# First cross-attention: parts of keys and queries kept in DRAM, core in chunks of four heads

## The chip, the cores and the metric

One core of a Trainium2 chip runs the kernel. The metric is the device time of one execution in microseconds; the time before is the median of three runs. The profile is one further execution.

## What is computed

A decoder of two layers on x of shape (2, 512, 512), each layer with self-attention, cross-attention to a context of shape (2, 1024, 512), and a mixture of experts. The change is in the cross-attention of the first layer:

```python
q = _qdq(x) @ _qdq(wq).T + bq            # int8 fake-quantised rows
kv = cond @ wkv.T + bkv
k, v = jnp.split(kv, 2, axis=-1)          # 16 heads of 32, 1024 keys, 512 queries, 2 batches
attn = jax.nn.softmax(jnp.einsum('bnhd,bmhd->bhnm', q, k) * scale, axis=-1)
o = jnp.einsum('bhnm,bmhd->bnhd', attn, v).reshape(B, N, C)
out = _qdq(o) @ _qdq(wp).T + bp
```

## The kernel before

The kernel is written engine by engine: SP, TensorE (pe), ScalarE (act), VectorE (dve) and GpSimd (pool) each have their own list of instructions in the order of the source, and wait for each other through counting semaphores. Every stage (`Stage`) ends with a barrier of all engines. The stages of the first cross-attention are `project_cross0` (projection), `attention_core` (the core) and `output_cross0` (output).

The projection makes keys transposed (`kt`, 128 rows of head features by 1024 keys, for each of 8 blocks of four heads), values (`v`), and queries (`qt`). Four context chunks of 512 tokens are multiplied by the key weights (L1025) and the value weights (L1033). Between them VectorE rounds the rows of the weights and of the normalised input (jobs, `round_rows`), ScalarE turns them into bf16 integers (L984), and after all four chunks TensorE transposes the 16 of them (L1041), ScalarE copies each away (L988), diagonal matmuls spread the scales (L1048), and the queries follow (L1057, L968, L1012). Keys are taken out of PSUM by L978, values by L937. Beside each head's 32 columns of values lie 32 columns of ones, written once, so that a matmul of 64 columns gives the weighted values and the sums of weights of one head.

Scores must be exact to more than float32r, so keys and queries are split into a high part (float32r, ScalarE, L704) and a low part (the rest, GpSimd, L746), and a score matmul contracts 96 rows: high by high, low query by high key, high query by low key. DMAs (L580 on SP for queries, L757 on GpSimd for keys) gather for each head these 96 rows from `parts` into `packed`, six transfers of each kind for a pair of heads; slots for four pairs exist.

The core then runs over 16 pair chunks j. First the maxima: `piece(j, n)` are two matmuls of 128 queries by 1024 keys of one head (L639), reduced by VectorE (`top`, L785), two pairs of PSUM banks taking turns. When eight are reduced, `turn` transposes the negated maxima (L645), ScalarE and VectorE make high and low rows of them (L710, L791), and SP puts the rows under the packed queries (L587, four transfers), beside rows of ones in the keys. So a second matmul (`scores`, L656, 98 rows, keys by queries) yields score minus maximum, ScalarE exponentiates (L718), and `values` (L668) multiplies with values and ones, two heads side by side in 64 columns each. In step kb of chunk j TensorE does the scores of block kb for two heads, the values of block kb-1, and one piece of chunk j+2. At the end of a chunk ScalarE copies the bank out (`take`, L724), SP moves values into `ot` and sums into `total` (L598, L599), and after every second chunk VectorE takes the reciprocal of 512 columns (L797) and multiplies (L799). VectorE's order is: top(j+2, 0), row(j+1), the other tops of j+2, then `norm` of the block before.

Of the kernel before, what the change touches and what calls it, by code (L numbers as in the profile page):

```python
# [15 lines left out]
P = 128  # L16
# [4 lines left out]
H = 16  # L21
# [492 lines left out]
def attention_core(nc, g, st, qt, kt, v, ot, nkt, masks=None):  # L514

    causal = masks is not None
    NI, NP, QB = B * KC, B * KC * HPC // 2, S // P
    NK = nkt * P
    KB = NK // S
    SLOTS = 4
    PB = 2 if causal else 1
    RING = 8
# [3 lines left out]
    parts = [st.sbuf(f"parts{n}", [P, 2 + 2 * KB, S], F32R) for n in range(PB)]  # L533
    packed = st.sbuf("packed", [P, SLOTS, 2, 1 + KB, S], F32R)
    probs = g.xt[:, :, :].rearrange("p k (a n) -> p (k a) n", n=S)
    nmax = st.sbuf("nmax", [P, 2, 2 * QB])
    rows = st.sbuf("rows", [2 * QB, 2, 2, P], F32R)
    osb = st.sbuf("osb", [P, 2, S])
    total = st.sbuf("total", [P, S])
    mask16 = st.sbuf("mask16", [P, P], BF16) if causal else None  # L540
    high_done, low_done = st.sem("high_done"), st.sem("low_done")
    packed_in = [st.sem(f"packed_in{n}") for n in range(SLOTS)]
    keys_in = [st.sem(f"keys_in{n}") for n in range(SLOTS)]
    rows_in = [st.sem(f"rows_in{n}") for n in range(2)]
    early_ones_done, late_ones_done = st.sem("early_ones_done"), st.sem("late_ones_done")
    mask_done = st.sem("mask_done")
# [4 lines left out]
    spread = [st.sem(f"spread{n}") for n in range(2)]  # L551
    inverted, normed = st.sem("inverted"), st.sem("normed")

    def high(u):
        t = parts[u % PB]
        return t[:, 0, :], t[:, 2:2 + KB, :].rearrange("p a n -> p (a n)")

    def low(u):
        t = parts[u % PB]
        return t[:, 1, :], t[:, 2 + KB:2 + 2 * KB, :].rearrange("p a n -> p (a n)")  # L560

    def piece_bank(j, n):
        return 2 * (((nkt + 1) * j + n) % 2)

    def start_of(kb):
        return kb * P if causal else 0

    with nc.Block() as block:
        @block.sync
        def _(sp):  # L570
            def pack(j):
                u, s = j // 2, j % SLOTS
                sp.wait_ge(low_done, 2 * u + 2)
                if j >= SLOTS:
                    sp.wait_ge(st_made, 2 * nkt * (j - SLOTS + 1))
                t = parts[u % PB]
                for h in range(2):
                    a = (2 * (j % 2) + h) * DH
                    for r, (qp, kp) in enumerate(TERMS):
                        sp.dma_start(packed[r * DH:(r + 1) * DH, s, h, 0, :].bitcast(F32),  # L580
                                     t[a:a + DH, qp, :].bitcast(F32)).then_inc(packed_in[s], 16)

            def put_rows(j):
                sp.wait_ge(row_low, j + 1)
                for n in range(2):
                    for h in range(2):
                        sp.dma_start(packed[KR + n:KR + n + 1, j % SLOTS, h, 0, :].bitcast(F32),  # L587
                                     rows[h * QB:(h + 1) * QB, j % 2, n, :].bitcast(F32)).then_inc(rows_in[j % 2], 16)

            def lay(j):  # L590
                i = j // 2
                sp.wait_ge(taken, j + 1)
                if j % 2 == 0 and i >= 1:
                    sp.wait_ge(normed, i)
                for h in range(2):
                    a = (2 * (j % 2) + h) * DH
                    val, ones = (3 if h else 0) * DH, (1 + h) * DH
                    sp.dma_start(ot[a:a + DH, i, :], osb[val:val + DH, j % 2, :]).then_inc(spread[j % 2], 16)  # L598
                    sp.dma_start(total[a:a + DH, :], osb[ones:ones + DH, j % 2, :]).then_inc(spread[j % 2], 16)  # L599

            for j in range(SLOTS):
                pack(j)
            put_rows(0)
            for j in range(NP):
                if j >= 1 and j + SLOTS - 1 < NP:
                    pack(j + SLOTS - 1)
                if j + 1 < NP:
                    put_rows(j + 1)
                if j >= 1:
                    lay(j - 1)  # L610
            lay(NP - 1)
            for n in range(2):
                sp.wait_ge(spread[n], 64 * NP // 2)

        @block.tensor
        def _(pe):
            def piece(j, n):
                s, bank = j % SLOTS, piece_bank(j, n)
                if n == 0:
                    pe.wait_ge(packed_in[s], PACK * (j // SLOTS + 1))  # L620
                    pe.wait_ge(keys_in[s], PACK * (j // SLOTS + 1))
                    if j >= 1:
                        pe.wait_ge(max_done, nkt * j)
                elif n == 1:
                    if j >= 1:
                        pe.wait_ge(row_low, j)
                else:
                    pe.wait_ge(max_done, nkt * j + n - 1)
                if causal:
                    w = (n + 1) * P  # L630
                    for h in range(2):
                        nc.tensor.matmul(g.ps[:, bank + h, 0:w], packed[0:KR, s, h, 0, n * P:(n + 1) * P],
                                         packed[0:KR, s, h, 1, 0:w], start=True, stop=False)
                        mm = nc.tensor.matmul(g.ps[:, bank + h, n * P:w], g.ident16[:, :], mask16[:, :], start=False,
                                              stop=True)
                else:
                    h, qb = divmod(n, QB)
                    for a in range(KB):
                        mm = nc.tensor.matmul(g.ps[:, bank + a, :], packed[0:KR, s, h, 0, qb * P:(qb + 1) * P],  # L639
                                              packed[0:KR, s, h, 1 + a, :], start=True, stop=True)  # L640
                mm.then_inc(max_made, 1)

            def turn(j):
                pe.wait_ge(max_done, nkt * (j + 1))
                nc.tensor.transpose(g.ps[0:2 * QB, piece_bank(j, nkt), 0:P], nmax[:, j % 2, :],  # L645
                                    g.ident[:, :]).then_inc(row_turned, 1)

            def scores(j, kb, h):
                s, e = j % SLOTS, 2 * (nkt * j + kb) + h
                if kb == 0 and h == 0:  # L650
                    pe.wait_ge(rows_in[j % 2], 64 * (j // 2 + 1))
                if e >= 2:
                    pe.wait_ge(exp_done, e - 1)
                a = start_of(kb)
                c = kb % QB * P
                mm = nc.tensor.matmul(g.ps[:, 4 + h, a:S], packed[0:KR + 2, s, h, 1 + kb // QB, c:c + P],  # L656
                                      packed[0:KR + 2, s, h, 0, a:S], start=True, stop=not causal)
                if causal:
                    mm = nc.tensor.matmul(g.ps[:, 4 + h, a:a + P], mask16[:, :], g.ident16[:, :], start=False, stop=True)
                mm.then_inc(st_made, 1)  # L660

            def values(j, kb):
                e, a = 2 * (nkt * j + kb), start_of(kb)
                pe.wait_ge(exp_done, e + 2)
                if kb == 0 and j >= 2:
                    pe.wait_ge(taken, j - 1)
                for h in range(2):
                    nc.tensor.matmul(g.ps[2 * h * DH:2 * (h + 1) * DH, 6 + j % 2, a:S],  # L668
                                     v[:, j // (H // 2), kb, j % (H // 2), h:h + 2, :].rearrange("p a d -> p (a d)"),
                                     probs[:, (e + h) % RING, a:S], start=(kb == 0),  # L670
                                     stop=(kb == nkt - 1)).then_inc(pv_made, 1)

            if causal:
                pe.wait_ge(mask_done, 1)
            for n in range(nkt):
                piece(0, n)
            turn(0)
            for n in range(nkt):
                piece(1, n)
            pe.wait_ge(early_ones_done, 1)  # L680
            pe.wait_ge(late_ones_done, 1)
            for j in range(NP):
                for kb in range(nkt):
                    scores(j, kb, 0)
                    scores(j, kb, 1)
                    if kb == 0 and j + 1 < NP:
                        turn(j + 1)
                    if kb >= 1:
                        values(j, kb - 1)
                    elif j >= 1:  # L690
                        values(j - 1, nkt - 1)
                    if j + 2 < NP:
                        piece(j + 2, kb)
            values(NP - 1, nkt - 1)

        @block.scalar
        def _(act):
# [1889 lines left out]
```

## Time and profile before

| | us |
|---|---|
| median of three runs | 3433.76 (3432.29 to 3434.08) |
| profiled execution, its own time | 3445.77 |
| its span, first to last instruction | 3444.0 |
| stretch of the projection's block to the first instruction of the core | 300 to 435.65 |
| first scores of the core | 476.09 |
| mean granted TensorE clock over the span | 0.92 |

TensorE is busy for 86% of the span, VectorE for 37%, ScalarE and GpSimd for 29% each. Busy times are averages over six stages of a different nature; only the second of them is touched, and it is read from its own stretches. A granted clock of 1.0 is 2.4 GHz, 0.5 is 1.2 GHz.

### The profile page before, as it was taken

The page shows a single profiled execution, that of the slowest core. Times are in us where ns is not written, and L with a number is a line of the kernel's source. Part 1 is how long each engine was busy: PE and PEld are TensorE (multiplying, and loading weights), DVE is VectorE, ACT ScalarE, POOL GpSimd, SP SyncE. Part 2 cuts the span into 40 slices and gives each one's busy share as a digit, 9 for nine tenths or more (in the row PEclk, how much of TensorE's full clock was granted, in tenths as well). Part 3 has the DMA queues.
Part 4 walks back from the last instruction along what each step waited for, and adds up shares of the span by engine and source line. Part 5 has one row for each costly group of instructions (what it writes and reads, how often), then busy time and mean ns, then how long its engine had stood idle before and what let it go on. Part 6 is the DMA issues. An engine that isn't in the chain of part 4 may idle for free. (4 is left out here: it accounts for less than half of the span.)

```text
span 3444.0 us, 42500 instructions
## 1 busy us (share of the span) xinstructions
PE 2962.6 (86%) x14027; PEld 1856.9 (54%) x14030; DVE 1291.0 (37%) x2069; ACT 1005.3 (29%) x2352; POOL 995.4 (29%) x1007
## 2 busy tenths in 40 slices
PE   7888969995399598799969899999999557999997
PEld 3453423333388345488848745555544424777772
DVE  3573355554111317554442265555540311111114
ACT  1461235443011126433310044444430001222220
POOL 2360032211211205244412055555540051221216
PEclk9999979997599799999989999999999677999998
DMA  2332033311199414144434332212210004999996
GB/s 83 76 73 89 13 82 72 71 41 34 61 328 322 139 42 96 46 156 140 140 110 144 95 125 76 74 64 76 76 37 0 28 18 145 346 342 339 345 305 197
DMA packets 308356, 434.40 MB, mean 126 GB/s; under 512 B 39871, under 2 KB 173479, under 8 KB 308233
## 3 DMA queue, kind: packets, MB, share of 16 engines
q1 hardware_dynamic: 273160, 348.88, 32.2%
q0 software_dynamic: 20096, 56.68, 5.9%
q10 hardware_dynamic: 14976, 27.27, 2.2%
q8 instruction: 69, 1.13, 0.1%
q14 instruction: 55, 0.44, 0.0%
HBM read 308.78 MB, written 75.58 MB: 112 GB/s over the span
## 5 line engine op out<-in xcount | busy, mean ns | idle before, releaser
L1586 PE MATMUL ps<-moe_blocks_xgt,moe_blocks_w 128*128 128x128 f32 (+1 forms) x3072 | 364.5, 277 | 6.2 <-DMA moe_blocks_b1s<-rb_cols 4.2
L1586 PEld LDWEIGHTS ps<-moe_blocks_xgt,moe_blocks_w 128*128 128x128 f32 (+1 forms) x3072 | 350.7, 185 | 10.8 <-issue 8.3
L2465 POOL TENSOR_TENSOR normed<-normed,xa_core_rinv 128x257 f32<-128x257 f32 (+1 forms) x256 | 265.8, 1061 | 273.2 <-DVE xa_core_rinv L2396 273.2
L1568 PE MATMUL ps<-moe_blocks_w,moe_blocks_ht 128*128 128x512 f32 (+1 forms) x624 | 285.0, 593 | 0.0
L2432 ACT ACTIVATE normed<-ps,xa_core_nmax 128x257 f32<-128x257 f32 (+1 forms) x256 | 173.6, 685 | 321.6 <-DVE xa_core_nmax L2391 321.1
L2391 DVE TENSOR_REDUCE xa_core_nmax<-ps 128x1 f32<-128x257 f32 (+1 forms) x256 | 164.5, 683 | 250.1 <-PE ps L2342 250.0
L2342 PE MATMUL ps<-xa_core_k,xa_core_q 128*128 128x512 f32 x512 | 242.3, 597 | 13.4 <-DVE xa_core_k L2381 11.6
L1657 DVE COPY moe_blocks_y<-ps 128x512 f32<-128x512 f32 x104 | 71.9, 691 | 454.9 <-PE ps L1568 454.9
L510 POOL TENSOR_TENSOR sa_w<-sa_w,sa_core_rinv 128x256 f32<-128x256 f32 (+3 forms) x128 | 159.2, 1253 | 239.5 <-DVE sa_core_rinv L457 239.5
L2368 PE MATMUL ps<-xa_core_pt,xa_core_v 128*128 128x512 f32 x512 | 225.1, 593 | 0.7 <-DVE xa_core_pt L2404 0.7
L785 DVE TENSOR_REDUCE xa_core_nmax<-ps 128x1 f32<-128x1024 f32 x128 | 155.9, 1223 | 138.1 <-PE ps L639 138.1
L718 ACT ACTIVATE normed<-ps 128x512 f32<-128x512 f32 x256 | 138.9, 595 | 160.1 <-PE ps L656 159.9
L2356 PEld LDWEIGHTS ps<-identity,normed 128*128 128x128 f32 x1024 | 118.2, 141 | 104.2 <-issue 67.8
L2121 POOL TENSOR_TENSOR normed<-normed 128x512 f32<-128x512 f32 x96 | 126.3, 1317 | 139.1 <-DVE normed L2081 139.1
L2356 PE MATMUL ps<-identity,normed 128*128 128x128 f32 x1024 | 146.3, 276 | 22.3 <-ACT xa_core_pt L2442 21.4
L1568 PEld LDWEIGHTS ps<-moe_blocks_w,moe_blocks_ht 128*128 128x128 f32 (+1 forms) x624 | 111.0, 191 | 100.2 <-issue 100.2
L1534 POOL COPY moe_blocks_idx<-moe_index 128x1 uint32 (+1 forms) x104 | 19.0, 183 | 490.2 <-PE ps L1559 437.2
L487 ACT ACTIVATE sa_w<-ps,sa_core_nmax 128x128 f32<-128x128 f32 (+3 forms) x256 | 132.2, 523 | 81.4 <-DVE sa_core_nmax L453 80.2
L1607 ACT ACTIVATE moe_blocks_xgt<-ps 128x512 f32<-128x512 f32 x104 | 62.1, 597 | 319.6 <-PE ps L1559 318.9
L2368 PEld LDWEIGHTS ps<-xa_core_pt,xa_core_v 128*128 128x128 f32 x512 | 95.0, 191 | 107.9 <-issue 107.0
L412 PE MATMUL ps<-identity,sa_w 128*128 128x128 f32 x640 | 122.0, 300 | 31.3 <-DVE normed L466 17.1
L668 PE MATMUL ps<-normed,xa_v 128*64 128x512 f32 x512 | 146.1, 651 | 0.0
(284 smaller groups left out, 5291.8 us busy)
## 6 DMA issues: line engine op xcount, KB each, us to landing
moe_blocks_w<-L_ffn_rw SPq DMA_DIRECT2D x80, 704.0 KB
moe_blocks_w<-L_ffn_rw SPq DMA_DIRECT2D x80, 512.0 KB
moe_blocks_w<-L_ffn_w SPq DMA_DIRECT2D x24, 1408.0 KB
moe_y<-moe_blocks_y ACTq DMA_DIRECT2D x104, 256.0 KB
sa_packed<-sa_parts SPq DMA_DIRECT2D x192, 128.0 KB
k_raw<-xa_kq_raw SPq DMA_DIRECT2D x64, 256.0 KB, 2.0
v_rows<-normed SPq DMA_DIRECT2D x64, 256.0 KB
xa_core_k<-k_raw SPq DMA_DIRECT2D x32, 512.0 KB, 4.7
```

The costliest lines, as they stand in the source:

```text
L510: nc.gpsimd.tensor_tensor(prob[:, 2 * s:2 * s + 2, 0:n], prob[:, 2 * s:2 * s + 2, 0:n], rinv[:, s, :, 0:1].to_broadcast([P, 2, n]), ALU.mu ...
L668: nc.tensor.matmul(g.ps[2 * h * DH:2 * (h + 1) * DH, 6 + j % 2, a:S], v[:, j // (H // 2), kb, j % (H // 2), h:h + 2, :].rearrange("p a d - ...
L718: nc.scalar.activation(probs[:, e % RING, a:S], g.ps[:, 4 + h, a:S], ACT.Exp).then_inc(exp_done, 1)
L785: nc.vector.tensor_reduce(nmax[:, j % 2, n:n + 1], g.ps[:, bank:bank + 2, :].rearrange("p a n -> p (a n)"), X_AXIS, ALU.max, negate=True). ...
L1568: mm = nc.tensor.matmul(g.ps[:, 6 + s % 2, :], ht[0:fn, s % 2, f, :], w2s[s][0:fn, f, :], start=(f == 0), stop=(f == NF - 1))
L1586: mm = nc.tensor.matmul(g.ps[0:fn, 2 + s % 2 + 2 * half, f * P:(f + 1) * P], w1s[s][:, k, half * F + f0:half * F + f0 + fn], xgt[:, s % 2, ...
L2342: mm = nc.tensor.matmul(s_ps(n)[:, c:c + 512], q[:, s, qb * P:(qb + 1) * P], k[:, s, c:c + 512], start=True, stop=True)
L2356: mm = nc.tensor.transpose(g.ps[:, 4 + half, m * P:(m + 1) * P], prob[:, nn % PR, c:c + P], g.ident[:, :])
L2368: mm = nc.tensor.matmul(g.ps[:, 6 + hs, :], v[:, hs, m, :], pt[:, hs, m, :], start=(m == 0), stop=(m == NKT - 1))
L2391: ins = nc.vector.tensor_reduce(nmax[:, n % PR, m:m + 1], s_ps(n)[:, lo:hi], X_AXIS, ALU.max, negate=True)
L2432: ins = nc.scalar.activation(prob[:, n % PR, lo:hi], s_ps(n)[:, lo:hi], ACT.Exp, bias=nmax[:, n % PR, m:m + 1], accum_out=rsum[:, n % PR, ...
L2465: ins = nc.gpsimd.tensor_tensor(prob[:, n % PR, lo:hi], prob[:, n % PR, lo:hi], rinv[:, n % PR, m:m + 1].to_broadcast([P, hi - lo]), ALU.mult)
```

## The change

The high and low parts are no longer made in the core. In the projection each key tile (one of 16) and query tile (one of 8) is written to `raw`, ScalarE copies it to `high`, GpSimd subtracts (`low`), all in rings of three, and SP stores both parts to DRAM (`k_parts`, `q_parts`). The last chunk's key and value matmuls are placed between the transposes. The core (`cross_core`) runs over 8 chunks of four heads. A chunk is loaded by six DMAs on SP, each with 32 rows for all four heads; there are three slots. Per block of keys there are four scores; the pieces of the next chunk, 16 of them, are placed three to a block. Values and totals use separate matmuls of 32 columns, four heads side by side, into two banks; ScalarE copies both out itself, and the reciprocal is cut into four and placed between reductions. The rows of maxima take two transfers instead of four. The rows of ones in the packed keys are written by GpSimd. `attention_core` was used only here and goes.

```diff
+def cross_core(nc, g, st, k_parts, q_parts, v, ot):
+    SLOTS = 3
+    STEPS = 2
+    PCS = HPC * QB
+    EACH = -(-PCS // (nkt - 1))
...
+            def pack(i):
+                s = i % SLOTS
+                if i >= SLOTS:
+                    sp.wait_ge(st_made, HPC * nkt * (i - SLOTS + 1))
+                for r, (qp, kp) in enumerate(TERMS):
+                    sp.dma_start(pq[r * DH:(r + 1) * DH, s, :, :].bitcast(F32),
+                                 q_parts[qp, i, :, :].rearrange("(h p) n -> p h n", p=DH)).then_inc(packed_in[s], 16)
+                    sp.dma_start(pk[r * DH:(r + 1) * DH, s, :, :].bitcast(F32),
+                                 k_parts[kp, i, :, :].rearrange("(h p) n -> p h n", p=DH)).then_inc(packed_in[s], 16)
...
+            pack(0)
+            pack(1)
             put_rows(0)
+            for i in range(NI):
+                if i + SLOTS - 1 < NI:
+                    pack(i + SLOTS - 1)
+                if i + 1 < NI:
+                    put_rows(i + 1)
...
+            def piece(i, m):
+                s, bank = i % SLOTS, piece_bank(i, m)
+                if m == 0:
+                    pe.wait_ge(packed_in[s], PACK * (i // SLOTS + 1))
+                    if i >= 1:
+                        pe.wait_ge(max_done, PCS * i)
+                elif m == 1:
+                    if i >= 1:
+                        pe.wait_ge(row_low, i)
                 else:
+                    pe.wait_ge(max_done, PCS * i + m - 1)
...
+                for h in (2 * pair, 2 * pair + 1):
+                    e = HPC * (nkt * i + kb) + h
+                    if e >= 2:
+                        pe.wait_ge(exp_done, e - 1)
+                    nc.tensor.matmul(g.ps[:, 4 + h % 2, :], pk[0:KR + 2, s, h, kb * P:(kb + 1) * P],
+                                     pq[0:KR + 2, s, h, :], start=True, stop=True).then_inc(st_made, 1)
...
+            def values(i, kb):
+                step = nkt * i + kb
+                b, c = divmod(i, KC)
+                pe.wait_ge(exp_done, HPC * step + HPC)
+                if kb == 0 and i >= 1:
+                    pe.wait_ge(taken, 2 * i)
+                for h in range(HPC):
+                    nc.tensor.matmul(g.ps[h * DH:(h + 1) * DH, 6, :], v[:, b, kb, c * P + h * DH:c * P + (h + 1) * DH],
+                                     probs[:, HPC * (step % STEPS) + h, :], start=(kb == 0), stop=(kb == nkt - 1))
+                for h in range(HPC):
+                    mm = nc.tensor.matmul(g.ps[h * DH:(h + 1) * DH, 7, :], g.ones[:, 0:DH],
+                                          probs[:, HPC * (step % STEPS) + h, :], start=(kb == 0), stop=(kb == nkt - 1))
+                mm.then_inc(pv_made, 1)
...
                 for kb in range(nkt):
+                    ahead = range(min(PCS, EACH * kb), min(PCS, EACH * (kb + 1))) if i + 1 < NI else ()
+                    if i == 0:
+                        for m in ahead:
+                            piece(i + 1, m)
+                    if kb == nkt - 1 and i + 1 < NI:
+                        turn(i + 1)
+                    scores(i, kb, 0)
+                    if i > 0:
+                        for m in ahead:
+                            piece(i + 1, m)
+                    scores(i, kb, 1)
                     if kb >= 1:
+                        values(i, kb - 1)
+                    elif i >= 1:
+                        values(i - 1, nkt - 1)
...
+                for m in range(PCS if i + 1 < NI else 0):
+                    top(i + 1, m)
+                    if i >= 1 and m in (6, 8, 10, 12):
+                        invert(i - 1, (m - 6) // 2)
+                    if i >= 1 and m == 14:
+                        norm(i - 1)
...
# project_cross0
+                sp.wait_ge(high_done, u + 1)
+                sp.dma_start(dst[0], high[:, u % HELD, :].bitcast(F32)).then_inc(stored[u % HELD], 16)
+                sp.wait_ge(low_done, u + 1)
+                sp.dma_start(dst[1], low[:, u % HELD, :].bitcast(F32)).then_inc(stored[u % HELD], 16)
...
+            for r in range(HELD):
+                sp.wait_ge(stored[r], 32 * len(range(r, UNITS, HELD)))
...
+            def held(u):
+                if u >= HELD:
+                    act.wait_ge(low_done, u - HELD + 1)
+                    act.wait_ge(stored[u % HELD], 32 * (u // HELD))
+                return raw[:, u % HELD, :]
+
+            def keep_high(u):
+                nc.scalar.activation(high[:, u % HELD, :], raw[:, u % HELD, :], ACT.Copy).then_inc(high_done, 1)
...
+                nc.scalar.activation(held(KU + j), qs[:, j % 2, :], ACT.Identity, bias=bqss[:, c:c + 1],
                                      scale=DH ** -0.5).then_inc(q_done, 1)
+                act.wait_ge(q_done, j + 1)
+                keep_high(KU + j)
...
+                if n % 2 == 0:
+                    if n // 2 < KC:
+                        key(NCH - 1, n // 2)
+                    else:
+                        value(NCH - 1, n // 2 - KC)
```

## Rows read from the trace of the kernel before

**Rows 1.** The page, part 1: busy us, share, instructions.
```profile
PE 2962.6 (86%) x14027; PEld 1856.9 (54%) x14030; DVE 1291.0 (37%) x2069; ACT 1005.3 (29%) x2352; POOL 995.4 (29%) x1007
```

**Rows 2.** The core's loop as one stretch: length, busy per engine (instructions), granted clock, DMA share, GB/s.
```profile
476.00:762.00 286.00, 262.53 (x913) 105.85 (x913) 163.13 (x139) 140.97 (x266) 56.61 (x84) 0.93 0.30 62
```

**Rows 3.** Groups by line, 300 to 1000 us: busy, mean ns, idle before.
```profile
L785 DVE TENSOR_REDUCE xa_core_nmax<-ps 128x1 f32<-128x1024 f32 x128 | 155.9, 1223 | 138.1 <-PE ps L639 138.1
...
L746 POOL TENSOR_TENSOR xa_core_parts<-xa_qt,xa_core_parts 128x512 fp32r<-128x512 f32 x8 | 10.1, 1267 | 216.3 <-ACT xa_core_parts L704 216.3
```

**Rows 4.** Timeline of one step: start, length, engine, line, operation, count, idle before.
```profile
559.94 0.74 PE L639 MATMUL ps<-xa_core_packed 96*128 96x512 f32 x2
...
560.52 0.63 PE L656 MATMUL ps<-xa_core_packed 98*128 98x512 f32 x2
560.72 1.23 DVE L785 TENSOR_REDUCE xa_core_nmax<-ps 128x1 f32<-128x1024 f32 x1 [0.93 <-PE ps L639]
...
560.75 0.40 PE L656 MATMUL ps<-xa_core_packed 98*128 98x512 f32 x1
...
560.95 1.08 ACT L718 ACTIVATE normed<-ps 128x512 f32<-128x512 f32 x2 [1.07 <-PE ps L656]
...
561.08 1.08 PE L668 MATMUL ps<-normed,xa_v 128*64 128x512 f32 x4
...
562.09 0.74 PE L639 MATMUL ps<-xa_core_packed 96*128 96x512 f32 x2
```

**Rows 5.** Timeline of a hand-over between two chunks.
```profile
572.62 3.34 DVE L797 RECIPROCAL xa_core_total<-xa_core_total 128x512 f32<-128x512 f32 x1
...
578.07 0.73 PE L639 MATMUL ps<-xa_core_packed 96*128 96x512 f32 x2 [1.90 <-DVE xa_core_rows L791]
```

**Rows 6.** Timeline of the start-up of the core.
```profile
452.06 2.08 PE L639 MATMUL ps<-xa_core_packed 96*128 96x512 f32 x4 [18.81 <-DMA xa_core_packed<-xa_core_parts]
...
463.35 0.08 PEld L645 LDWEIGHTS ps<-identity,xa_core_nmax 128*8 128x8 f32 x1 [2.03 <-DVE xa_core_nmax L785]
...
472.31 8.09 SPq L587 DMA_DIRECT2D xa_core_packed<-xa_core_rows  x5
...
476.09 1.19 PE L656 MATMUL ps<-xa_core_packed 98*128 98x512 f32 x2 [2.70 <-DMA xa_core_packed<-xa_core_rows]
```

**Rows 7.** Timeline of the projection's end; one row of line L1012 (min/median/max ns).
```profile
386.76 13.90 PE L1025 MATMUL ps<-xa_proj_ctx,xa_proj_wkv 128*128 128x512 f32 x32
...
394.03 0.63 ACT L984 ACTIVATE xa_proj_wp_int<-xa_proj_rounded 128x512 bf16<-128x512 f32 x1 [0.23 <-DVE xa_proj_rounded L929]
...
423.07 0.66 PE L1048 MATMUL ps<-xa_proj_diag,all_ones 128*128 128x128 f32 x4
...
L1012 ACT ACTIVATE xa_qt<-xa_proj_rounded,xa_proj_bqss x8: 721/722/723, 428.2 to 434.1; 128x512 f32<-128x512 f32 x8
...
435.65 0.63 ACT L704 ACTIVATE xa_core_parts<-xa_qt 128x512 fp32r<-128x512 f32 x1 [0.85 <-PEq L67]
```

**Rows 8.** Self-attention: the values of 32 columns, timeline; its whole stretch.
```profile
163.30 1.08 PE L429 MATMUL ps<-normed,sa_v 128*32 128x128 f32 x32
...
124.00:268.00 144.00, 119.76 (x1234) 80.88 (x1235) 102.31 (x200) 91.72 (x303) 79.60 (x64) 0.94 0.31 67
```

**Rows 9.** DMA issues (KB, us to landing); stretches as in rows 2.
```profile
k_raw<-xa_kq_raw SPq DMA_DIRECT2D x64, 256.0 KB, 2.0
...
444.00:447.00 3.00, 0.00 (x0) 0.00 (x0) 0.00 (x0) 0.00 (x0) 3.00 (x7) 0.50 0.99 194
447.00:450.00 3.00, 0.00 (x0) 0.00 (x0) 0.00 (x0) 0.00 (x0) 0.24 (x1) 0.50 1.02 246
...
300.00:305.00 5.00, 3.01 (x4) 1.49 (x5) 3.49 (x1) 0.00 (x0) 3.51 (x1) 0.50 1.05 406
```

**Rows 10.** Timeline of the core's end.
```profile
788.61 0.60 ACT L724 ACTIVATE xa_core_osb<-ps 128x512 f32<-128x512 f32 x1 [1.20 <-PE ps L668]
...
796.52 0.69 DVE L799 TENSOR_TENSOR xa_qt<-xa_qt,xa_core_total 128x512 f32<-128x512 f32 x1
```

More of the change, by code:

```diff
@@ L550, in attention_core, with piece_bank @@
     pv_made, taken = st.sem("pv_made"), st.sem("taken")
-    spread = [st.sem(f"spread{n}") for n in range(2)]
     inverted, normed = st.sem("inverted"), st.sem("normed")
[L554 to L566, printed above, removed]
+    def piece_bank(i, m):
+        return 2 * (((PCS + 1) * i + m) % 2)
     with nc.Block() as block:
@@ new lines, in piece @@
+            def piece(i, m):
[7 more added lines that the diff above has]
+                        pe.wait_ge(row_low, i)
+                else:
+                    pe.wait_ge(max_done, PCS * i + m - 1)
+                h, qb = divmod(m, QB)
+                for a in range(KB):
+                    mm = nc.tensor.matmul(g.ps[:, bank + a, :], pq[0:KR, s, h, qb * P:(qb + 1) * P],
+                                          pk[0:KR, s, h, a * S:(a + 1) * S], start=True, stop=True)
@@ L641, in piece, with turn @@
                 mm.then_inc(max_made, 1)
-            def turn(j):
-                pe.wait_ge(max_done, nkt * (j + 1))
-                nc.tensor.transpose(g.ps[0:2 * QB, piece_bank(j, nkt), 0:P], nmax[:, j % 2, :],
+            def turn(i):
+                pe.wait_ge(max_done, PCS * (i + 1))
+                nc.tensor.transpose(g.ps[0:HPC * QB, piece_bank(i, PCS), 0:P], nmax[:, i % 2, :],
                                     g.ident[:, :]).then_inc(row_turned, 1)
[L648 to L671, printed above, removed]
@@ L694, in _, with scores @@
-            values(NP - 1, nkt - 1)
+            def scores(i, kb, pair):
+                s = i % SLOTS
+                if kb == 0 and pair == 0:
+                    pe.wait_ge(rows_in[i % 2], 32 * (i // 2 + 1))
+                for h in (2 * pair, 2 * pair + 1):
[4 more added lines that the diff above has]
+                                     pq[0:KR + 2, s, h, :], start=True, stop=True).then_inc(st_made, 1)
@@ new lines, in row, with invert @@
+            def row(i):
+                dve.wait_ge(row_high, i + 1)
+                nc.vector.tensor_tensor(rows[:, i % 2, 1, :], g.ps[0:HPC * QB, piece_bank(i, PCS), 0:P],
+                                        rows[:, i % 2, 0, :], ALU.subtract).then_inc(row_low, 1)
+            def invert(i, n):
+                if n == 0:
+                    dve.wait_ge(taken, 2 * i + 1)
+                part = slice(n * P, (n + 1) * P)
+                nc.vector.reciprocal(total[:, part], total[:, part]).then_inc(inverted, 1)
@@ L864, in project_cross0 @@
     qs = rounded
+    raw, low = st.sbuf("raw", [P, HELD, S]), st.sbuf("low", [P, HELD, S], F32R)
+    high = st.sbuf("high", [P, HELD, S], F32R)
+    high_done, low_done = st.sem("high_done"), st.sem("low_done")
+    stored = [st.sem(f"stored{n}") for n in range(HELD)]
     w_loaded = [st.sem("wq_loaded"), st.sem("wp_loaded")]
```

383 lines of the change are left out of this document (140 added, 243 removed).

## The prediction

> **What bounds the kernel now.** I read the busy shares of the page first: TensorE is the busiest engine by far [rows 1]. Then the stretches of the stage that is changed. In the projection TensorE runs its matmuls without a gap (32 in 13.90 us [rows 7]); at the start-up of the core, to 476, the clock stands at 0.50, the lower level of 1.2 GHz [rows 9]; from 476 to 762 TensorE is busy for 92% at a mean clock of 0.93 [rows 2]. The groups by line give the unit costs that will be moved around [rows 3]. The timeline of one undisturbed step of the loop [rows 4] shows what sets its length: two score pieces begin at 559.94, two scores at 560.52, the value group at 561.08, the next pieces at 562.09. That is 2.15 us with TensorE never waiting; VectorE and ScalarE finish their part and sit idle. So the inner step is bound by TensorE, and every wait that the change puts into TensorE's queue is paid in full. The hand-over between two pair chunks is different: a 3.34 us reciprocal stands on VectorE ahead of the row that TensorE wants, and TensorE waits for it [rows 5]. Two more places lie on the path: the start-up, where packed keys arrive only at 452.06, then reductions set the pace, and the rows' transfers are issued only at 472.31 because the 24 transfers of queries stand ahead of them on SP [rows 6]; and the end of the projection, where queries leave at 0.82 us each [rows 7].
>
> Unit times I take from these rows. A float32r matmul of 512 columns: the next one starts 0.23 to 0.24 later (560.52, 560.75); the first after a float32 group or a wait takes 0.34 (0.58 less 0.24). From the start of the last matmul of a piece to its reduction 0.44, the reduction 1.22, back to TensorE 0.05. From a score to its exponential 0.43 (0.53 if it is the first), the exponential 0.60, a pitch of 0.5. Values of two heads: 1.01 for two passes of 0.43 side by side, with 0.15 for the start and the end.
>
> **Projection, moved work.** Each of 24 tiles (16 of keys, 8 of queries) now gets a high part on ScalarE (0.63, as L984 [rows 7]), a low part on GpSimd (1.27 [rows 3]) and two stores of 256 KB (2.0 us from issue to landing, the rows of the other DRAM buffer [rows 9]), in a ring of three. For keys this is hidden: a key tile comes every 3.43 us (eight records of 0.43 in [rows 7]), while the ring turns over in 0.72 + 0.63 + 1.27 + 0.15 for semaphores + 2.0 to 2.6 for issue and landing = about 5.1 us for three tiles. If that cover were gone, it would be 1.7 us a tile. For the eight queries nothing covers it: three tiles per 5.1 us, the last starting 11.6 us in and landing at 16.7, and SP waits for every store before the stage ends. Today the eight take 6.6 (428.2 to 434.8). So +10.1.
>
> The transposes are moved between the last keys and values. TensorE reaches them at 386.76. The third needs ScalarE's first copy, which stands behind the four roundings that end at 394.66 [rows 7]: a wait of 4.3 us. Then 16 transposes of 0.4 and 8 groups of 3.43 give 386.8 + 4.3 + 6.4 + 27.5 = 425.0, and the last value bias and the diagonals follow on VectorE before the row matmuls at 425.9, against 423.07 now: +2.8. The copies that used to pace the transposes are hidden, but their gain is eaten by the wait and by the diagonals that come late. The core stage then begins at 435.65 + 10.1 + 2.8 = 448.6.
>
> **Start-up of the core.** Removed: the high and low parts and 24 + 24 small transfers. Added: six loads for the first chunk, 3 x 256 + 3 x 512 KB = 2.36 MB, issued at once. Their rate is not in the trace in this form. Bounds: 194 to 246 GB/s when pairs are packed onto 32 partitions, 406 GB/s for wide loads from DRAM [rows 9]; 12 or 6 us. I take 225 GB/s, 10.5 us, since the 32 destination partitions and 2 to 4 KB pieces are the same as in the packing row. With 2.0 latency and 0.3 to begin, chunk 0 is there at 461.4 (now 452.06; the load itself is quicker than today's 16.4). Then 16 pieces run one behind the other, each 1.27 (eight take 11.3 until the transpose, [rows 6]): transpose at 482.8, row ready 1.0 later, two row transfers 2.6, first scores at 486.4. Today they start at 476.09. So +10.3: the 12.9 from the projection less 2.6. The Trainium skill, page DMA: Bandwidth & Descriptors (section Anatomy of one DMA), gives 2.0 us plus bytes at 436 GB/s; that would make it 7.4 us instead of 12.5, and the forecast 5 us lower. The packing row speaks against it, at half that rate with the engines' share near one.
>
> **The loop.** Per block of 128 keys and four heads there are now 4 scores, three pieces (6 matmuls) in blocks 0 to 4, one in block 5, none in 6 and 7, and eight 32-column float32 matmuls (four values, four of ones). Whether four groups of 32 columns run side by side is shown by the self-attention: 32 records of 128 columns, eight groups of four, in 1.08 us with the last one's tail [rows 8]. One record of 512 columns is 0.43 [rows 7], so one of 128 is 0.11, and eight of these make 0.87: the four in a group cost as much as one. Values and ones: 0.48 + 3 x 0.43 + 0.10 = 1.87. The upper bound is twice today's group, 2.02 (+9 us over 64 blocks); the lower 4 x 0.43 = 1.72.
>
> A block with three pieces, from its first score: scores at 0 and 0.34; first piece at 0.58 and 0.82; second at 1.06 and 1.30. The third uses the banks of the first, whose reduction runs from 1.26 to 2.48: it starts at 2.53 and not at 1.53, a wait of 1.0. Scores of the other pair at 3.11 and 3.35 (their exponentials are long done), the values' group from 3.68 to 5.55. VectorE needs 3 x 1.2 plus at most 1.7 of quarter reciprocals in that time, so it keeps up. A block without pieces: the third score waits for the first exponential (0.53 + 0.60 + 0.05 = 1.18) and the fourth for the second (1.67), the group from 2.1 to 3.97. A chunk is 5 x 5.55 + 3 x 3.97 + 0.1 for the transpose = 39.8; today two pair chunks cost 16 x 2.15 = 34.4 of bare steps and then their hand-overs, some 40.8. The first chunk, where pieces stand ahead of both score pairs and cover neither exponential, is 43.0, the last 34.4. Sum 43.0 + 6 x 39.8 + 34.4 = 316; I add 2 for the first block or two at half clock: 318. Today 788.6 - 476.1 = 312.5. So +5.5. What goes: the wait of the row behind the reciprocal [rows 5], about 2 us at seven hand-overs, and the half clock that follows it. What comes: the third piece's wait, 35 x 1.0, and 23 us of waits for exponentials. Rows that land in 4 us instead of 2.6 would add 6.
>
> **Tail.** Now from the last values (788.6) over four transfers, reciprocal and product to 797.2: 8.7 [rows 10]. New: copy of the totals 0.6, four quarter reciprocals 3.5 (0.84 and a gap each, a quarter of 3.34), product 0.7, semaphores 0.2 = 5.0. So -3.7.
>
> **Sum.** 10.3 + 5.5 - 3.7 = +12.1 us. The profiled execution took 3445.8 (span 3444.0), 12.0 over the median of the timed runs, 3433.8; the difference is carried over to the median: 3446.
>
> **Rivals.**
> A, the clock: TensorE now waits 1.0 us in most blocks. For it: the page's clock of 0.93 in 476 to 762 shows dips right after waits of 1 to 2 us. Against it: self-attention has more idle time (TensorE busy for 83% from 124 to 268 us) at a mean clock of 0.94 [rows 8]. At half clock a three-piece block takes 10 x 0.43 + 4 x 0.86 + 0.2 = 7.9 instead of 5.55. If as much of the loop is slow as now (7% by the mean of 0.93 means 14%, some 45 us), that is 45 x (1 - 5.55/7.9) = 13 us more: 3459. The Trainium skill, page TensorE: Matmul & The Clock Gate (section A second HAM failure mode), says that frequent short idles between groups of matmuls make the clock swing; by it the dips would come in every chunk, and this rival would be the likeliest. So far the self-attention's rows don't bear it out.
> B, quick transfers, the case that ends not slower: stores land in about 1 us, so that ScalarE (1.4 a tile) and no longer the ring paces the queries, 13.5 instead of 16.7; and chunk 0 loads at 400 GB/s, 4.6 less. It decides from a store under about 1.6 us on. 12.1 - 7.8 = +4: 3438, no change that can be told.
> C, the third piece's wait is hidden: if reductions end before TensorE comes back, 35 us less, of which the quarter reciprocals return some; 12 - 30 = -18: 3416. For it only that VectorE has room over a chunk (24 of 40 us); against it, two bank pairs and a reduction of 1.22 that outlasts two pieces.
> D, the four-wide groups don't overlap fully when totals follow values in the same columns: 2.02 or more, +9 and up: 3455. Against it [rows 8].
>
> **Chances.** Forecast 0.45 (its own range 3439 to 3455), A 0.17, D 0.10, B 0.15, C and other gains 0.13. A measurement of this kernel can tell about 0.2%, 7 us, from no change. Slower by more: 0.71 (forecast, A, D less a little of the forecast's low edge, 0.01); within: 0.16; faster: 0.13. The range, 3430 to 3464, reaches over B below and A above and leaves out C.
>
> **What would show it.** Right: core stage from about 449, packed keys at 461, first scores at 486, chunks of 40 us, blocks of 5.5 and 4.0, TensorE waiting for the reduction once in each three-piece block (35 times some 1.0) and for exponentials in the others, output stage from 810. Wrong: queries of the projection spaced by under 1.5 us; chunks under 38 or over 43; a clock well under 0.93 in the loop; a third piece that doesn't wait.

## The result and the profile after

The new kernel takes 3446.3 us (median, 3440.1 to 3452.6) against 3433.6 (3425.2 to 3434.1) for the kernel before in the same session: ratio 1.0036, 95% interval 1.0022 to 1.0051, so 8 to 18 us slower. Forecast: 3446. One execution of one later version (keys of the first chunk early) took 4521 us at a mean granted clock of 0.64 and is left out.

The two profiled executions end only 0.7 us apart (spans 3444.7 and 3444.0), and that difference must not be read. The cause is far behind the change, in the second mixture. Here is that stretch as one window, with the columns of [rows 2], first of the kernel before:

```profile
2781.00:2867.00 86.00, 57.39 (x112) 21.33 (x112) 5.82 (x8) 4.11 (x6) 46.05 (x48) 0.80 0.07 17
```

and of the kernel after:

```profile
2795.00:2861.00 66.00, 53.96 (x112) 20.34 (x112) 6.00 (x8) 4.11 (x6) 46.04 (x48) 0.89 0.09 23
```

The same 112 matmuls take 20 us less. Most of that, 16.6 us, is idle time: in the profiled execution of before TensorE stands still three times between its matmuls at 2822 and 2848, the last time for 17.4 us, and in that of after it doesn't (busy 57.4 and 54.0). The experts' stage behind them, the same 2745 matmuls, takes 508 us in place of 499. Neither is touched by the change. What the change did is read from times inside its own two stages. All of them stand 1.5 us late in the profiled execution of after, since the first projection matmul starts at 303.53 and not at 301.99; I take these 1.5 off below.

The end of the projection and the hand-over to the core, as a timeline:

```profile
395.95 0.59 PE L1006 MATMUL ps<-identity,xa_proj_wq_int 128*128 128x128 bf16 x4 [4.43 <-ACT xa_proj_wqt L941]
396.33 6.46 PE L980 MATMUL ps<-xa_proj_ctx,xa_proj_wkv 128*128 128x512 f32 x8
...
407.01 3.65 PE L980 MATMUL ps<-xa_proj_ctx,xa_proj_wkv 128*128 128x512 f32 x8
...
427.38 0.71 PE L1018 MATMUL ps<-xa_proj_diag,all_ones 128*128 128x128 f32 x4 [0.76 <-DVE xa_proj_diag L899]
...
432.54 0.72 ACT L968 ACTIVATE xa_proj_raw<-xa_proj_rounded,xa_proj_bqss 128x512 f32<-128x512 f32 x1 [1.21 <-DVE xa_proj_rounded L908]
...
437.48 0.72 ACT L968 ACTIVATE xa_proj_raw<-xa_proj_rounded,xa_proj_bqss 128x512 f32<-128x512 f32 x1 [0.99 <-DMA xa_q_parts<-xa_proj_low]
...
442.46 0.72 ACT L968 ACTIVATE xa_proj_raw<-xa_proj_rounded,xa_proj_bqss 128x512 f32<-128x512 f32 x1 [0.90 <-DMA xa_q_parts<-xa_proj_low]
...
446.85 0.32 SPq L830 DMA_DIRECT2D xa_q_parts<-xa_proj_low  x1
450.31 0.32 SPq L553 DMA_DIRECT2D xa_core_pq<-xa_q_parts  x1
```

The first row is the wait of 4.4 us for ScalarE's copy. Towards its end the granted clock falls to 0.5, for 6.8 us from 395.1 on, and the eight matmuls behind it take 6.46 us where the next eight take 3.65. The queries leave in threes: after each third tile a gap that a store ends. The core's first load is issued at 450.31, where [rows 7] had the stage begin at 435.65. Its start-up, against [rows 6]:

```profile
463.58 2.07 PE L588 MATMUL ps<-xa_core_pk,xa_core_pq 96*128 96x512 f32 x4 [25.98 <-DMA xa_core_pk<-xa_k_parts]
...
485.03 0.38 PE L594 MATMUL ps<-identity,xa_core_nmax 128*16 128x128 f32 x1 [1.32 <-DVE xa_core_nmax L695]
...
486.06 1.21 SPq L561 DMA_DIRECT2D xa_core_pq<-xa_core_rows  x2
...
488.66 0.72 PE L605 MATMUL ps<-xa_core_pq,xa_core_pk 98*128 98x512 f32 x1
```

One block of the loop, TensorE alone, against the step in [rows 4]:

```profile
533.88 0.73 PE L605 MATMUL ps<-xa_core_pq,xa_core_pk 98*128 98x512 f32 x2
534.46 1.09 PE L588 MATMUL ps<-xa_core_pk,xa_core_pq 96*128 96x512 f32 x4
536.40 0.73 PE L588 MATMUL ps<-xa_core_pk,xa_core_pq 96*128 96x512 f32 x2 [0.86 <-DVE xa_core_nmax L695]
536.97 0.64 PE L605 MATMUL ps<-xa_core_pq,xa_core_pk 98*128 98x512 f32 x2
537.54 1.06 PE L615 MATMUL ps<-normed,xa_v 128*32 128x512 f32 x8
538.42 1.04 PE L618 MATMUL ps<-normed,all_ones 128*32 128x512 f32 x8
539.39 0.72 PE L605 MATMUL ps<-xa_core_pq,xa_core_pk 98*128 98x512 f32 x2
```

The block is 539.39 - 533.88 = 5.51 us. Two pieces follow each other at once; the third waits 0.86 for the reduction that frees its banks. Values and totals, 16 records, take 1.85. The loop as a window (columns of [rows 2]), and waits from 489 to 806 (waiter, what it waits for, us in total, times, longest; PEld is TensorE's loading of weights, which waits ahead of the matmul):

```profile
489.00:763.00 274.00, 237.39 (x1290) 99.11 (x1289) 153.15 (x146) 124.73 (x235) 0.00 (x0) 0.97 0.26 52
```

```profile
PEld ps L605 <- ACT normed L660: 63.4, 98, 1.5
PEld ps L588 <- DVE xa_core_nmax L695: 43.6, 34, 1.3
...
PE ps L588 <- DVE xa_core_nmax L695: 28.8, 34, 0.9
```

TensorE waits for a reduction 34 times, some 0.85 each: 30 times in the six middle chunks and four times in the first. And the end of the core, against [rows 10]:

```profile
805.81 0.60 ACT L667 ACTIVATE xa_core_total<-ps 128x512 f32<-128x512 f32 x1 [3.00 <-PE ps L618]
...
806.44 3.39 DVE L708 RECIPROCAL xa_core_total<-xa_core_total 128x128 f32<-128x128 f32 x4 [27.39 <-ACT xa_core_total L667]
809.86 0.69 DVE L713 TENSOR_TENSOR xa_ot<-xa_ot,xa_core_total 128x512 f32<-128x512 f32 x1
```

### The profile page after: what moved, and what is told of

The parts are those of the page before. It is cut to its first block and busy times, and to the rows that moved or that the text cites. A ratio compares the mean times of both kernels' runs of the same rounds, so it can differ in the third digit from the quotient of the medians.

```text
span 3444.7 us, 43271 instructions
## 1 busy us (share of the span) xinstructions
PE 2958.4 (86%) x14531; PEld 1856.2 (54%) x14534; DVE 1277.6 (37%) x2084; ACT 1007.2 (29%) x2352; POOL 952.4 (28%) x919
## 5 line engine op out<-in xcount | busy, mean ns | idle before, releaser
L2312 PE MATMUL ps<-xa_core_k,xa_core_q 128*128 128x512 f32 x512 | 243.8, 599 | 12.7 <-DVE xa_core_k L2351 11.8
L2312 PEld LDWEIGHTS ps<-xa_core_k,xa_core_q 128*128 128x128 f32 x512 | 90.8, 193 | 92.6 <-issue 77.7
```

What stands on the lines that cost most here:

```text
L2312: mm = nc.tensor.matmul(s_ps(n)[:, c:c + 512], q[:, s, qb * P:(qb + 1) * P], k[:, s, c:c + 512], start=True, stop=True)
```

## The experiments

The first four ran in one session (the kernel before there: 3427.0 us), the last four in another (3450.6). Only ratios to the kernel before of the same session are compared. The block times below run from the first scores of one block to those of the next.

**Third piece behind the values.** After the values' matmuls TensorE comes to the third piece late enough for its banks to be free.

```
-  for m in ahead:          # ahead of the second pair of scores
+  for m in ahead[:2]:
 ...
+  for m in ahead[2:]:      # behind values and totals
+      piece(i + 1, m)
```

> The changed kernel with one edit in TensorE's order: from the second chunk on, the third piece of a block comes after the values' group and no longer between the two pairs of scores. Theory (the third piece's wait for the reduction of the first is paid in full, 1.0 us in each of 30 blocks): blocks with three pieces go from 5.50 to about 4.5 us, 30 us off the loop, median some 3416. Rival (these waits only stand in for VectorE's pace or return as another wait): blocks stay over 5.2, time within 5 us of 3446. Second rival (the clock decides): time moves with the share at half clock, not with the wait.

Measured: 3424.6 us, ratio 0.9991 (0.9982 to 1.0001), against 1.0036: 15 us gained, half of the 30 expected. A chunk takes 36.45 in place of 39.4. One and a half blocks of it:

```profile
568.67 0.74 PE L605 MATMUL ps<-xa_core_pq,xa_core_pk 98*128 98x512 f32 x2
569.26 1.09 PE L588 MATMUL ps<-xa_core_pk,xa_core_pq 96*128 96x512 f32 x4
570.18 0.67 PE L605 MATMUL ps<-xa_core_pq,xa_core_pk 98*128 98x512 f32 x2
570.78 1.07 PE L615 MATMUL ps<-normed,xa_v 128*32 128x512 f32 x8
571.66 1.04 PE L618 MATMUL ps<-normed,all_ones 128*32 128x512 f32 x8
572.63 0.74 PE L588 MATMUL ps<-xa_core_pk,xa_core_pq 96*128 96x512 f32 x2
573.22 0.63 PE L605 MATMUL ps<-xa_core_pq,xa_core_pk 98*128 98x512 f32 x2
573.68 0.63 PE L588 MATMUL ps<-xa_core_pk,xa_core_pq 96*128 96x512 f32 x2
574.70 0.50 PE L588 MATMUL ps<-xa_core_pk,xa_core_pq 96*128 96x512 f32 x1 [0.38 <-DVE xa_core_nmax L698]
```

The first block is 4.5 us, the later ones 5.03: in the next block the second piece waits for the banks of the late third (574.70). So the wait was real and on the path. Moving it gives back 2.95 of the five waits' 4.3 us in a chunk, two thirds; the rest comes back one block later. The first chunk's four waits were not moved.

**At most two pieces between the scores.** Two pieces in each of the first five blocks, three in the sixth and the seventh, the third of them behind the values. The edit also gives the first chunk this order, but for its first block; in the new kernel its pieces stand ahead of all scores and cover no exponential.

```
-  EACH = -(-PCS // (nkt - 1))
+  AT = [0, 2, 4, 6, 8, 10, 13, 16, 16]    # pieces of the next chunk done before block kb
```

> The changed kernel with the pieces spread 2, 2, 2, 2, 2, 3, 3 over seven blocks instead of 3, 3, 3, 3, 3, 1: two always between the pairs of scores, a third behind the values; the first chunk like the others but for its first block. Theory (two waits are paid separately: third piece, and exponentials where no piece covers them): blocks with two pieces 4.0 us, with three 4.5, a chunk 33.2 instead of 39.4, the first one some 37 instead of 45; in all 45 to 50 us less, median near 3398, below the kernel before. Rival (VectorE, with 16 reductions, four quarter reciprocals and a product, becomes the pace at 24 us a chunk plus its latencies): chunk above 36.

Measured: 3417.3 us, ratio 0.9963 (0.9950 to 0.9977). Four blocks of a chunk are at 3.96 and two at 4.54, but the seventh takes 6.56 and the eighth in five of seven chunks 5.2 to 5.6: chunks of 35.4 to 37.1 where 33.2 was expected. The first chunk takes 35.9 in place of 45.2. The hand-over:

```profile
591.47 0.73 PE L588 MATMUL ps<-xa_core_pk,xa_core_pq 96*128 96x512 f32 x2
...
593.52 0.28 PE L594 MATMUL ps<-identity,xa_core_nmax 128*16 128x128 f32 x1 [1.32 <-DVE xa_core_nmax L698]
...
595.63 1.87 PE L615 MATMUL ps<-normed,xa_v 128*32 128x512 f32 x8
...
597.26 1.95 PE L618 MATMUL ps<-normed,all_ones 128*32 128x512 f32 x8
...
599.14 0.73 PE L605 MATMUL ps<-xa_core_pq,xa_core_pk 98*128 98x512 f32 x2
...
601.24 1.06 PE L615 MATMUL ps<-normed,xa_v 128*32 128x512 f32 x8
```

The last piece stands at 591.47, its reduction ends at 593.46, and the turn of the maxima waits for it; behind this idle time the same eight matmuls take 1.87 in place of 1.06, the lower clock. My expectation left out that the last piece must be early enough for the turn.

**The kernel before with its reciprocal in quarters.** Nothing of the change; the one reciprocal of 512 columns per chunk becomes four of 128 between the reductions of the next steps.

```
-  nc.vector.reciprocal(total[:, :], total[:, :]).then_inc(inverted, 1)
-  dve.wait_ge(inverted, i + 1)
+  dve.wait_ge(inverted, 4 * (i + 1))
 ...
+  if 2 <= n <= 5:
+      invert((j - 1) // 2 - 1, n - 2)     # one quarter a step
```

> The kernel before with only VectorE's reciprocal cut into four quarters that stand between the reductions of the next odd chunk, and the product behind them. Theory (the kernel before loses about 2 us of wait at seven hand-overs and then runs at half clock for a while): hand-over steps of 4.09 fall to about 2.2, chunks with dips of 20 to 25 us fall to 18.4; 20 to 28 us less, median near 3409. Rival (the dips have another cause, such as the load itself): only 14 us or less, steps of 3.9 stay.

Measured: 3410.9 us, ratio 0.9939 (0.9925 to 0.9952): 21 us gained. First its hand-over, against [rows 5]; then, as windows, the same 14 pair chunks in the kernel before and in this one, each from its first scores on:

```profile
555.23 0.27 PE L645 MATMUL ps<-identity,xa_core_nmax 128*8 128x128 f32 x1 [0.84 <-DVE xa_core_nmax L785]
555.43 1.08 PE L668 MATMUL ps<-normed,xa_v 128*64 128x512 f32 x4
556.44 0.72 PE L639 MATMUL ps<-xa_core_packed 96*128 96x512 f32 x2
```

```profile
476.09:759.67 283.58, 261.05 (x906) 105.35 (x907) 161.67 (x137) 139.62 (x263) 56.61 (x84) 0.93 0.30 63
480.38:737.41 257.03, 245.63 (x907) 99.76 (x907) 162.70 (x155) 139.63 (x263) 56.61 (x84) 0.99 0.31 68
```

What took 283.6 us takes 257.0; TensorE is busy for 245.6 in place of 261.1, so 15.4 of the 26.6 us are matmuls at the lower clock. The rest are waits: six hand-overs (the prediction says seven) with 1.9 us each. The timed runs gained 21 (16 to 26). In the kernel before it is a hand-over like this one that the time goes to:

```profile
537.91 0.72 PE L639 MATMUL ps<-xa_core_packed 96*128 96x512 f32 x2 [1.90 <-DVE xa_core_rows L791]
538.47 0.83 PE L656 MATMUL ps<-xa_core_packed 98*128 98x512 f32 x2
539.24 1.97 PE L668 MATMUL ps<-normed,xa_v 128*64 128x512 f32 x4
```

The edit does two things at once: it cuts the reciprocal, and it moves it from ahead of the row of maxima to behind it. Whether the move alone would do was not run. What the change brought into its loop as a gain was to be had without the change, and it hid how much the rest of the change costs: against this kernel the new one is 1.0036/0.9939, 33 us slower.

**Old order of the projection.** The new kernel with all transposes in one row behind the last values, as they were before.

```
-  for n in range(NCH - 1):
+  for n in range(NCH):
 ...
-  if n % 2 == 0:           # a key or value group between the transposes
```

> The changed kernel with the projection's order put back: all four context chunks first, then the 16 transposes in a row. Theory (the interleaving costs 2.8 us, since TensorE waits 4.4 for the first copy and the diagonals come late): the first diagonal matmul 3 us earlier and the core stage begins at about 447 instead of 449.8. Rival (the copies that then pace the transposes cost as much as the wait): no difference, within 0.5 us.

Measured, one execution: 3449.0 us. Its stage starts 1.2 us later than that of after, so the first diagonals (425.73) are 2.8 earlier than there, as expected. But the queries gain only 1.4:

```profile
420.68 1.17 PE L1002 MATMUL ps<-identity,xa_proj_x_int 128*128 128x128 bf16 x8 [0.19 <-ACT xa_proj_xqt L941]
...
425.73 4.70 PE L1009 MATMUL ps<-xa_proj_diag,all_ones 128*128 128x128 f32 x16
```

In the row of transposes the clock fell to half at 420.1 for 10.2 us, and the 16 diagonal products take 4.70 us, 3.3 in after. The order alone doesn't settle this: the kernel before has the same row of transposes and ran it at full clock, its sibling with the quartered reciprocal at half. And in all seven runs with the new order the clock falls too, at the end of the wait of 4.43 us, for 3.4 to 6.8 us. From the first matmul of the stage to the first query it is 126.2, 127.6 and 127.6 us in the three runs with the old order and 127.8 to 129.0 in the seven with the new one, of which after is the slowest: the reordering costs some 1.3 us on the mean, and 2.8 between the two kernels compared.

**Five held parts in place of three.**

```
-  RING, HELD = 2, 3
+  RING, HELD = 2, 5
```

> The new kernel with five held parts in place of three (HELD 5) in the projection stage, nothing else. Theory: the queries' products wait for the DMA of a store to release a held tile (raw gaps of about 0.9 to 1.0 us in front of them, ended by DMA xa_q_parts from xa_proj_low). With five tiles these gaps go; by the product of gaps and their number the core stage starts 2 to 3 us earlier than in the new kernel (its start mark then stands 11 to 12 us behind that of the kernel before, stage offset included, against 14.6), and everything behind it is unchanged. Rival: the stores themselves are the bound; then more tiles only let the products run ahead, the last store lands when it did and the core stage starts within 1 us of where it does in the new kernel. One look only: the total will not tell 3 us from scatter, the stage marks will.

Measured, one execution: 3464.6 us, a total too uncertain for 2 us. By its stages, the queries start at 431.84 and the last at 440.78, 1.28 apart without a gap; the core's first load is issued 16.2 us after the first query, 17.8 in after:

```profile
431.84 0.72 ACT L968 ACTIVATE xa_proj_raw<-xa_proj_rounded,xa_proj_bqss 128x512 f32<-128x512 f32 x1 [1.21 <-DVE xa_proj_rounded L908]
...
440.78 0.71 ACT L968 ACTIVATE xa_proj_raw<-xa_proj_rounded,xa_proj_bqss 128x512 f32<-128x512 f32 x1
```

The ring costs 1.6 us, then, less than the 2 to 3 expected. Counted from the first matmul of the stage its core starts 2.8 us earlier than in after, but the other 1.2 lie ahead of the queries, where the clock was at half for 3.4 us in place of 6.8. What remains is ScalarE at 1.28 a tile and the last landing.

**Third pieces early.** As the second experiment, with the third pieces in the first and the third block of a chunk (the expectation calls them the second and the fourth), so that the last piece stands ahead of the values of the seventh block and no longer behind them.

```
+  AT = [0, 3, 5, 8, 10, 12, 14, 16, 16]
```

> The loop of the kernel with two pieces between the score pairs, the third pieces moved: the second and the fourth block of a chunk take a third piece behind the values, and the last block has none, so that the turn of the next chunk finds its last reduction finished. Theory: a block with two pieces between its score pairs costs 3.97 us, a block with a third behind the values 4.54, and the 6.6 us block before the hand-over as well as the half clock behind it were the wait of the turn for the last reduction alone. A chunk is then 6 x 3.97 + 2 x 4.54 = 32.9 us, against 35.4 to 37.1 with the third pieces late and 39.4 in the new kernel; the stage is 7 x 6.5 = 45 us shorter than the new one's, about 3399 us at a base of 3433, ratio about 0.990. Rival: the granted clock falls to half at the hand-over for another reason (the first exponentials of a chunk are waited for anyway); then the first block stays at 5.4 to 5.6 in most chunks, a chunk is 34.5, and the ratio stays near 0.9935.

Measured: 3420.6 us, ratio 0.9909 (0.9891 to 0.9927). Blocks 4.53, 4.47, 4.53, 4.48, 3.96, 3.95, 4.29, 3.93: a chunk of 34.1 (32.9 expected, since the blocks behind a late third are 4.5 as well, as in the first experiment). The first chunk takes 33.8 in place of 45.2. The half clock behind the hand-over is gone; what is left is one fall of 3.4 us in the last chunk:

```profile
490.00:761.00 271.00, 256.38 (x1475) 111.10 (x1474) 158.29 (x152) 146.74 (x276) 0.00 (x0) 0.98 0.26 53
```

So it hung on the turn's wait, as the theory said, and the rival falls. One chunk's eighth block takes 4.67 in place of 3.93 at full clock: TensorE waits 0.66 us for the transfer of the rows of maxima.

**Keys of the first chunk loaded during the projection.** The loop is that of the sixth experiment.

```
+  if n == 1:               # both halves of the first key rows are stored
+      for r, kp in enumerate((0, 0, 1)):
+          sp.dma_start(pk0[r * DH:(r + 1) * DH, :, :].bitcast(F32), k_parts[kp, 0, ...]).then_inc(keys0, 16)
```

> The same loop, and the packed keys of chunk 0 (three of its six loads, 1.57 of 2.36 MB) are loaded in the projection stage, behind the second context chunk, into a tile that outlives it; at the start of the core stage chunk 0 has its queries alone to load. Theory: the 13.3 us between the issue of the first packed loads and the first product of the core stage are the transfer of the chunk's 2.36 MB at the rate of this pattern; with the queries alone (a third of it) they become about 2.0 + 11.3/3 = 5.8, so 7.5 us less than the kernel with the same loop, ratio lower by 0.0022, and nothing in the projection stage slows. Rival: the 13.3 us are mostly a fixed cost of the queue for its first loads, or the loads in the projection stage hold up the context loads or the stores by a few us: gain under 3 us.

Measured: five executions of 3406.4 to 3418.7 us, ratio 0.9885 (0.9864 to 0.9906), 0.0024 under the one before it: 8 us, but the two intervals overlap, and it is the trace that shows the gain. The loads of 0.79 MB are issued at 451.08:

```profile
456.52 2.07 PE L592 MATMUL ps<-xa_pk,xa_core_pq 96*128 96x512 f32 x4 [17.89 <-DMA xa_core_pq<-xa_q_parts]
```

5.4 us, against 463.58 - 450.31 = 13.3 for 2.36 MB: 1.57 MB cost 7.8 us, 200 GB/s. The early loads didn't make the projection longer: 128.2 us from its first matmul to the first query, in the middle of the 127.8 to 129.0 of the seven runs.

**All of it.** The same with five held parts.

> All of it: the loop with the third pieces early, the keys of chunk 0 loaded early, and five held parts in the projection stage. Theory: the parts add, since each acts in another stretch: 2 to 3 us less than the kernel with early keys, about 3389 us at a base of 3433, ratio 0.987. Rival: the load of chunk 0's queries waits for the last store, which lands when it did, and nothing is won over the kernel with early keys.

Measured: 3408.4 us, ratio 0.9884 (0.9865 to 0.9904), the same as without the fifth part: 1.6 us can't be told apart in totals. It is, with the one before it, the quickest version: 0.9884 against 0.9939 for the old core with quartered reciprocals and 1.0036 for the change as made. The last comparison crosses sessions.

## Why the prediction was right, point by point

- **Projection, +12.9 forecast.** The core's first load is issued at 450.31 - 1.5 = 448.8; forecast 448.6. The transposes' share is 427.38 - 423.07 - 1.5 = 2.8, as forecast, and the wait in front of them 4.4 (4.3). That the sum comes out to a tenth is luck: the eight matmuls behind the wait took 2.8 us more than others, at the lower clock, which the forecast didn't have, and the transposes took 0.25 each where it had 0.4, 2 us less. Over seven runs of this order the share lies between 1.6 and 2.8. The queries' share, 10.1, held as well, in groups of three tiles (1.3 apart in a group, 1.65 on the mean; under 1.5 was to be the sign of being wrong). But its reason was too narrow: I held the ring for the cause, and with five tiles only 1.6 us go. The rest is work that the parts put on ScalarE and the last store's landing, which no ring removes; that is read from the trace, and no run takes them out.
- **Start-up.** The first piece comes 13.3 us after the issue (12.8), the first scores at 487.1 (486.4): +11.1 for +10.3. The rate taken from the packing row, 225 GB/s, was close to the 200 measured. The Trainium skill, page DMA: Bandwidth & Descriptors (section Anatomy of one DMA), gives 2.0 us plus bytes at 436 GB/s for one transfer issued by GpSimd; these loads are six, or three, issued by SP. An estimate by the page's sum is 7.4 us for 2.36 MB and 3.8 for 0.79 MB; the runs measured 13.3 and 5.4. For this pattern it is too quick.
- **Loop, +5.5.** From the first scores to the end of the last values 805.8 - 488.7 = 317.1; forecast 318, so +4.6. Blocks of 5.51 and 3.96 (5.55 and 3.97), chunks of 39.4 (39.8), 34 waits of 0.85 (35 of 1.0), values and totals 1.85 (1.87), no wait at the hand-over. The first chunk took 45.2 where I had 43 + 2, the last 35.6 (34.4), with the clock at half for 3.4 us from 777.4 on. The small sum hides large parts, and they are seen one by one: the third piece's wait is 29 us (34 x 0.86), of which the simplest move gave back 15; the other way, the old hand-over's waits and lower clock were 21 in the timed runs and 26.6 in the profiled ones.
- **Tail, -3.7.** From the last values 810.55 - 805.8 = 4.7 us (5.0), 3.9 less than before.
- **Sum.** 11.1 + 4.6 - 3.9 = +11.8 (12.1); the timed ratio gives +12 with 8 to 18.
- **Rows of maxima.** The prediction put +6 us on rows that land in 4 us instead of 2.6. In after no chunk waited for them; in the fourth, sixth and eighth experiment single chunks did, by 0.66 to 1.24 us. So the margin is thin, and why a transfer is late now and then stays open.
- **Rival A,** the clock: it didn't fall as feared: 0.97 in the loop, with TensorE busy for 87%, where the kernel before had 0.93 and 92%; past the start-up it was at half twice, for 3.4 us each, in the first chunk (504.4) and in the last. The Trainium skill, page TensorE: Matmul & The Clock Gate (section A second HAM failure mode), has frequent short idles swing the clock; here a wait of 0.86 in five of eight blocks left it at full speed through six chunks. What fell to half followed a wait of 1.9 in the kernel before, at five of six hand-overs, and one of 1.32 in the second experiment, at five of seven.
- **Rival B,** quick stores: no, the queries' stores landed in 2.2 to 2.4 us (median), with 0.9 us gaps ended by stores.
- **Rival C,** a hidden third piece: no, but the experiments that hide it show its price was right in kind: 15 us for the simplest move, 44 for the full reordering (1.0036 less 0.9909, across sessions). Of the 44, 11.4 are the first chunk's (45.2 to 33.8), whose pieces now also cover the exponentials; the six middle chunks gave 5.3 each.
- **Rival D,** four groups that don't overlap: no. Values 0.88 (537.54 to 538.42) and totals 0.97 (538.42 to 539.39), as forecast.

## What to carry to other kernels

A block that is bound by TensorE pays for each wait for PSUM banks, as here 0.86 us for each third piece. With two pairs of banks, don't put three pieces in a row: spread them so that TensorE comes back to a pair after other work, and end them one block before their result is wanted. When a change brings several small repairs with it, try each on the old kernel: here the quartered and moved reciprocal alone was worth 21 us there, and the rest of the change cost 33. For a transfer, the rate of a row with the same destination partitions and piece size was a better guide here than the rate of wide loads.

## What the runs showed of the hardware

- One reciprocal of 128 x 512 (3.34 us) on VectorE cost the old loop its full length and more: TensorE waited 1.9 behind it at six hand-overs, and at five of them the clock was then at the lower of its two levels for 3.4 to 10.2 us, 26.6 us in all in the profiled execution. Four of 128 columns (0.94 each), behind the row and with reductions in between, removed both: granted clock 0.99 in place of 0.93.
- The same code met the lower clock at different places in different executions. The loop of the fourth experiment is that of after, yet one chunk took 42.4 us where all of after's six took 39.4: TensorE waited 0.77 us for the rows of maxima at its start, and the clock was at half for 6.8 us from 655.7 on. Another took 40.7 at full clock, and that was a wait for the same transfer, issued at 732.23:

```profile
736.58 0.73 PE L605 MATMUL ps<-xa_core_pq,xa_core_pk 98*128 98x512 f32 x2 [1.24 <-DMA xa_core_pq<-xa_core_rows]
```

Single stage times of this kernel are thus sure to a few us only; why the clock fell and the transfer was late stays open.
- Packed loads onto 32 partitions each moved 200 GB/s, half of the 406 in [rows 9], with the next chunk's loads queued right behind.
